# Output part of test-time training: VectorE's three chains of a step woven into each other, and the turn of the block's norm moved behind the output projection

## The reference, cut to what matters

```
Z1_bar = xq @ W1_s - eta_mb * Attn1 @ grad + b1_bar     # Attn1 = tril(xq @ xk.T)
out = xq + _ln(Z1_bar, ln_w, ln_b)                      # norm over the 8 features of a head
...
out = _ln(out, post_norm_weight, post_norm_bias)        # "post norm", over 256 features
return out @ o_w.T                                      # output projection
...
x = _layernorm(x + _L0_attn_ref(x, ...), axis=-1)       # the block's norm, over 256 features
```

## Time and profile before

| what | value |
|---|---|
| median of 3 runs | 1165.35 us |
| the three runs | 1157.6, 1166.76, 1165.35 us |
| span of the profiled execution (first to last instruction) | 1158.9 us |
| share of the span busy: TensorE, weight load, VectorE, ScalarE, GpSimd | 91%, 57%, 73%, 50%, 23% |
| first score matmul of step 0 | 169.31 us |
| first matmul of the next stage | 306.36 us |
| mean granted TensorE clock over the span | 0.975 |

### The profile page before, as it was taken

The page is one execution under the profiler, slowest core; times in us unless marked ns, Lnnn a source line. Parts: engine busy times, 40 slices in busy tenths (PEclk is TensorE's granted clock), DMA queues, the critical chain, the costliest instruction groups (busy, mean ns, idle before and its releaser), DMA issues. The chain is left out here.

```text
span 1158.9 us, 24222 instructions
## 1 busy us (share of the span) xinstructions
PE 1055.9 (91%) x8933; PEld 656.8 (57%) x8947; DVE 840.8 (73%) x1995; ACT 579.6 (50%) x1574; POOL 268.3 (23%) x331
## 2 busy tenths in 40 slices
PE   9799989999899999898999978899999998899965
PEld 5467757777433333354555457677777776444432
DVE  3699978999868778589984997854487878833326
ACT  2446444544267667654442336477777775322212
POOL 5201001111201112224422110410000001167742
PEclk9999999999899999999999989999999999999977
DMA  6833332000222221710000002940000000869567
GB/s 194 138 92 103 107 108 77 2 2 2 74 64 88 83 82 56 124 36 1 1 1 1 2 1 99 304 135 20 19 20 20 24 20 23 255 174 229 86 132 276
DMA packets 79200, 94.82 MB, mean 82 GB/s; under 512 B 17504, under 2 KB 61478, under 8 KB 78822
## 3 DMA queue, kind: packets, MB, share of 16 engines
q1 hardware_dynamic: 69356, 78.67, 23.8%
q0 software_dynamic: 6496, 9.57, 4.4%
q10 hardware_dynamic: 3232, 5.03, 1.2%
HBM read 68.65 MB, written 21.97 MB: 78 GB/s over the span
## 5 line engine op out<-in xcount | busy, mean ns | idle before, releaser
L533 DVE TENSOR_REDUCE gqa_x_slots<-banks 128x8 f32<-128x1024 f32 x64 | 78.4, 1226 | 28.9 <-PE banks L424 19.7
L490 ACT ACTIVATE gqa_expT<-banks 128x1024 f32<-128x1024 f32 x64 | 65.6, 1025 | 50.6 <-PE banks L445 50.6
L1752 ACT ACTIVATE mla_probs<-mla_scores,mla_neg_max 128x128 f32<-128x128 f32 x256 | 90.5, 386 | 0.1
L786 PE MATMUL banks<-ff_x_parts,ff_w_gate_up 128*128 128x512 bf16 x370 | 87.6, 384 | 1.9 <-PEq L348 1.2
L1825 DVE TENSOR_REDUCE mla_neg_max<-mla_scores 128x8 f32<-128x1024 f32 x32 | 39.2, 1225 | 64.9 <-PE mla_scores L1650 38.5
L445 PE MATMUL banks<-gqa_x_slotsT,gqa_keys 32*128 32x512 f32 x256 | 73.7, 646 | 13.2 <-issue 4.0
L424 PE MATMUL banks<-gqa_keys_bd,xT 32*128 32x512 f32 x256 | 72.6, 653 | 0.6 <-DVE gqa_x_slots L533 0.3
L1640 PE MATMUL mla_q_ps<-xT,mla_merged_home 128*128 128x128 f32 x512 | 62.4, 275 | 0.0
L786 PEld LDWEIGHTS banks<-ff_x_parts,ff_w_gate_up 128*128 128x128 bf16 x384 | 37.8, 99 | 42.5 <-issue 3.4
L1677 PE MATMUL mla_out_ps<-mla_merged_home,mla_attT 128*128 128x256 f32 x256 | 60.7, 380 | 0.7 <-ACT mla_attT L1766 0.7
L1640 PEld LDWEIGHTS mla_q_ps<-xT,mla_merged_home 128*128 128x128 f32 x512 | 59.7, 192 | 0.0
(11 more groups left out here) (448 smaller groups left out, 2580.4 us busy)
## 6 DMA issues: line engine op xcount, KB each, us to landing
gqa_keys_bd<-in_gqa_keys_bd SPq DMA_DIRECT2D x16, 512.0 KB, 3.4
moe_w_gu<-in_moe_w_gu SPq DMA_DIRECT2D x14, 384.0 KB, 5.7
moe_w_dn<-in_moe_w_down SPq DMA_DIRECT2D x24, 192.0 KB, 5.8
moe_sums<-moe_zeros SPq DMA_DIRECT2D x2, 2176.0 KB, 10.4
ba_attended<-in_moe_w_gu SPq DMA_DIRECT2D x10, 384.0 KB, 4.6
x_tok<-in_mla_kv_wo SPq DMA_DIRECT2D x8, 320.0 KB, 3.8
ttt_by_token<-ttt_g_pairs SPq DMA_DIRECT2D x4, 576.0 KB, 4.7
ttt_lanes<-ttt_by_token SPq DMA_DIRECT2D x16, 144.0 KB, 6.1
```

The lines of the kernel that those rows point to most:

```text
L490: nc.scalar.activation(expT[:, k % 2, 2 * u:2 * u + 2, :], scoresT, ACT.Exp, scale=HD ** -0.5).then_inc(exp_ready, 1)
L533: nc.vector.tensor_reduce(x_slots[:, b % 2, :, c * NJ + 2 * half:c * NJ + 2 * half + 2, HD].rearrange("p g j -> p j g"), scores[:, of].rea ...
L786: ins = nc.tensor.matmul(tile[:, n % 2], w_up[:, c, k, f * P:(f + 1) * P], x_parts[:, g % 2, part, c, :], start=(c == 0 and part == 0), st ...
L1752: ins = nc.scalar.activation(probs[:, k % NB, e, i, :], scores[:, k % 2, e, i, :], ACT.Exp, bias=neg_max[:, k % 2, e, i:i + 1], accum_out= ...
```

## The change

VectorE's step is written out by hand. Two methods are added to `Order`: `mark` raises the semaphore and returns the count to wait for, `after` waits for such a count. So the instruction that makes a result and the one that needs it can stand apart, and instructions of the other two chains stand between them. The head norm's chain moves ahead of masks 3 but for its last three instructions; the variance's reduction moves ahead of masks 2; the post norm is written ahead of the block norm's variance, and the block norm is written behind masks 2. The product with gamma is taken before the product with the reciprocal root. `added` and step 16's `block_norm` get a wait for `norm.turn_copied`, and `residual`'s wait becomes `resT_copied` in place of `resT_ready`.

TensorE issues `norm.tensor(b-3)` in unit 3, behind `last.out(b-2)`, and no longer in unit 2 ahead of `last.turn_res(b-2)` (but for b = 16, where it stays in unit 2, behind `turn_res`). ScalarE's order becomes `deviation`, `copy_res`, `norm.scalar`. No instruction that computes is added or dropped.

```
+    def mark(self, ins):
+        ins.then_inc(self.sem, 1)
+        self.k += 1
+        return self.base + self.k
+    def after(self, count):
+        self.eng.wait_ge(self.sem, count)
...
-                    if b == B + 1:
+                    if live(b - 2):
                         deviation(b - 2)
+                    if live(b - 3):
+                        last.copy_res(act, b - 3)
                     if live(b - 4):
                         norm.scalar(act, b - 4)
-                    if live(b - 3):
-                        last.copy_res(act, b - 3)
-                    if live(b - 2) and b != B + 1:
-                        deviation(b - 2)
...
                         if u == 2 and b == B:
                             last.turn_res(pe, b - 2)
-                        if u == 2 and live(b - 3):
+                        if u == 2 and live(b - 3) and b == B:
                             norm.tensor(pe, b - 3)
...
                         if u == 3 and live(b - 2) and b < B:
                             last.out(pe, b - 2)
+                        if u == 3 and live(b - 3) and b < B:
+                            norm.tensor(pe, b - 3)
...
                         post_stats(b - 2)
+                        need(dve, norm.turn_copied, b - 3)
                         block_norm(b - 3)
...
+                    masks(b, 0)
+                    if live(b - 2):
+                        need(dve, q_read, b - 1)
+                        post_summed = order.mark(nc.vector.bn_stats(last.stats[:], res))
+                    if live(b - 3):
+                        if b == 3:
+                            dve.wait_ge(x_loaded, 16)
+                        need(dve, last.out_ready, b - 2)
+                        need(dve, norm.turn_copied, b - 3)
+                        added = order.mark(norm.added(b - 3, last.out_of(b - 3)))
+                    if live(b - 2):
+                        order.after(post_summed)
+                        nc.vector.memset(last.spare[:], 0.0)
+                        post_spread = order.mark(nc.vector.bn_aggr(last.mean_var[:], last.stats[:]))
+                    if live(b - 3):
+                        order.after(added)
+                        summed = order.mark(nc.vector.bn_stats(norm.stats[:], norm.total))
+                    if live(b - 2):
+                        order.after(post_spread)
+                        ts(last.var_eps[:], last.mean_var[:, 1:2], last.EPS, None, ALU.add).then_inc(last.post_var_ready, 1)
+                    masks(b, 1)
+                    if live(b - 3):
+                        order.after(summed)
+                        nc.vector.memset(norm.spare[:], 0.0)
+                        spread = order.mark(nc.vector.bn_aggr(norm.mean_var[:], norm.stats[:]))
+                    if live(b - 2):
+                        post_norm(b - 2)
+                    if live(b - 3):
+                        order.after(spread)
+                        ts(norm.var_eps[:], norm.mean_var[:, 1:2], LN_EPS, None, ALU.add).then_inc(norm.var_ready, 1)
+                    if live(b - 1):
+                        need(dve, squared, b)
+                        tr(var[:], sq[:], AX_X, ALU.add).then_inc(var_ready, 1)
+                    masks(b, 2)
+                    if live(b - 1):
+                        need(dve, var_ready, b)
+                        order.mark(ts(head_var_eps[:], var[:], 1.0 / HD, EPS, ALU.mult, ALU.add))
+                        need(dve, std_ready, b)
+                        root = order.mark(nc.vector.reciprocal(rstd[:], std[:]))
+                        need(dve, z_kept, b)
+                        order.mark(tt(z[:].rearrange("p h d -> p (h d)"), z[:].rearrange("p h d -> p (h d)"), gamma_row[:], ALU.mult))
+                        order.after(root)
+                        half_square = order.mark(stt(spare_h[:], rstd[:], -0.5, rstd[:], ALU.mult, ALU.mult))
+                    if live(b - 3):
+                        need(dve, norm.rstd_ready, b - 2)
+                        need(dve, norm.kept, b - 3)
+                        need(dve, norm.turn_ready, b - 3)
+                        ts(norm.normed, norm.total, norm.mean_var[:, 0:1], norm.rstd[:], ALU.subtract, ALU.mult).then_inc(norm.norm_ready, 1)
+                    if live(b - 1):
+                        order.after(half_square)
+                        step_of = order.mark(tt(spare_h[:], spare_h[:], head_var_eps[:], ALU.mult))
+                    masks(b, 3)
+                    if live(b - 1):
+                        order.after(step_of)
+                        order(stt(rstd[:], spare_h[:], 1.5, rstd[:], ALU.add, ALU.mult))
+                        order(tt(z[:], z[:], wide(rstd), ALU.mult))
+                        need(dve, last.resT_copied, b - 1)
+                        need(dve, q_ready, b)
+                        tt(res, z[:].rearrange("p h d -> p (h d)"), q_tok_ps, ALU.add).then_inc(q_read, 1)
```

## The result

| | before | changed |
|---|---|---|
| median of 20 runs each, us | 1165.87 | 1158.75 |
| ratio to before (95% interval) | | 0.9942 (0.9924 to 0.9960) |
| span of the profiled execution, us | 1158.9 | 1160.2 (its own time 1162.08) |
| first score matmul of step 1 to the first matmul of the next stage, us | 173.50 to 306.36 = 132.86 | 175.83 to 303.50 = 127.67 |

The kernel became 0.6% faster, between 4.7 and 8.9 us. I had forecast 2.7 us. The time lies in the range, but the gain was about twice what I wrote (1.7 to 3.3 times), and most of what follows is about where that came from.

The account below looks back on a forecast made before the run. VectorE was taken to bound the step at 8.4 us, with TensorE needing 8.25. Gains of 1.0 (steps 3 to 15), 0.5 (step 2) and 1.2 (stage's end) made 2.7 us: 1165.35 to 1162.6, range 1154.5 to 1168.0 with run scatter.

Parts of the forecast that it names:

- The bound: Middle steps: VectorE sets 8.4 us, TensorE would need 8.25, so only about 0.15 us a step can be cashed.
- 11 x 0.12 = 1.3 us: VectorE's step: eleven of 14 waits for its own results go, each worth 0.12 us.
- 7.95 + 0.37 = 8.32: TensorE's new step: `norm.tensor` at 7.95 plus 0.37 to the next scores; range 8.25 to 8.48, against 8.40.
- 0.5 + 1.2: Stage's ends: 0.5 us gained in step 2 (0.3 to 0.6), 1.2 at step 16 and the end (0.9 to 1.6).
- the two cases that I had weighed: Stage's end, half-speed stretch behind step 16's stand: if it goes too, 1.6 us in all; if it stays, 0.9.
- The clock rival: Half-speed stretches here and in the next stage: 7 us less gives 3.5 us more than forecast, 1159.1; chance 0.1.
- The steps' own range: Whole kernel, without the scatter of runs: 1161.2 to 1165.2 us, a gain of 0.2 to 4.2.
- The slow rival: ScalarE's queue: a late reduction holds `copy_res` behind `deviation`, then `out` and TensorE wait; 5.2 us lost, 1167.9; chance 0.07.

Follow-up runs that it names:

- moves_only: Changed kernel with VectorE's old program (new waits kept) and `deviation` behind `copy_res`; TensorE's order as changed: 1164.97 us, ratio to before 1.0005.
- waits_at_once: Changed kernel with VectorE's new instruction order, but each own result waited for at once: 1160.99 us, ratio to before 0.9959.
- weave_only: Changed kernel with `norm.tensor` back ahead of `turn_res` and `norm.scalar` back ahead of `copy_res`: 1210.63 us, ratio to before 1.0329.
- after_again: Changed kernel once more with no edit, for a second profile and a comparison on one chip: 1159.35 us, ratio to before 0.9949.
- deviation_late: Changed kernel with ScalarE's `deviation` (square root) back behind `copy_res`: 1167.33 us, ratio to before 1.0000.

## Why the prediction was right in direction and too small in size

**The bound: right.** VectorE's own instructions set 8.4 us, TensorE would need less. Shown from both sides: the move alone leaves 8.42 (`moves_only`), and with the weave VectorE waits 1.02 us a step for TensorE.

**VectorE, "11 x 0.12 = 1.3 us": right.** `waits_at_once` puts these waits back, but for one (the block norm row's own wait stays away, the one behind `added` comes back), and VectorE needs 1.3 us a step more. What it had to spare in the changed kernel is nearly used up. The rows' reading (0.33 against 0.45) held, and the rule of the Trainium skill (VectorE: DVE Perf Modes, "The DRAIN you can't avoid"), that chains take as long with semaphores as without, did not hold for the instructions of 0.42 us here: 0.12 us each. That the time is nevertheless nearly the same with and without these waits is not that rule; it is TensorE's bound.

**TensorE's step, "7.95 + 0.37 = 8.32": this is the term that was mis-sized.** It measured 8.16, outside the 8.25 to 8.48 that I had given it. Up to `out` every offset was right to 0.01; the two spacings behind it were 0.96 and 0.31 in place of 1.06 and 0.37. I took `out` to scores for `out` to transposes, and gave as its other end a duration (1.13) on the longer side only. The lower side was left open, and it was there: the spacing between two groups belongs to the pair of neighbours, not to the first of them. Steps 3 to 15 gained 2.85 + 0.23 = 3.1 us, not 1.0.

**The ends of the stage, "0.5 + 1.2": 0.6 and 1.5.** Step 2 went from 8.54 to 7.95. In step 16 the stand went, and the clock stayed at 2.4 GHz, the better of the two cases that I had weighed: from the start of `apply(15,2)` to the hand-over it is 9.09 us before (297.27 to 306.36) and 7.58 after (295.92 to 303.50). In two profiles this stand is long (0.88 us before, 0.66 in `moves_only`), and the clock fell to half about 2 us behind it; in none of the eight in which it was gone or at most 0.6 us did it fall between the stand and the hand-over. `weave_only`, with its stands in every step, is left out of this count. That the stand is the cause is the likely reading of these rows, but it was not tested by itself. A window of `moves_only`, at 0.52:

```profile
302.10:305.50 3.40, 3.40 (x9) 1.75 (x8) 3.12 (x11) 0.73 (x3) 0.94 (x2) 0.52 0.00 0
```

**The sum.** 3.1 + 0.6 + 1.5 = 5.2 us in the stage, which lies in the interval of 4.7 to 8.9. The middle of that interval is 1.6 us more. Nothing outside the stage has changed, and single profiles differ by 4 us behind it. The clock rival had 1159.1, next to the measured 1158.75, but the clocks on record do not bear it out: among the runs that the ratio of `after_again` uses, the mean granted clock was 0.9743 changed and 0.9736 before, some 2 us less at half speed out of 60. That is worth 1 us and lies within the scatter. (The one stretch of 3.4 us that went with the stand of step 16 is already in the 1.5.) The mean times of these runs differ by 5.5 us, close to the stage's 5.2. So most of the 1.6 us is likely scatter, though this is not shown for the batch of the main result.

That the time lies between 1154.5 and 1168.0 was no proof of the sum: this range was the scatter of the runs, and no gain at all would have been inside it too. The steps' own range, a gain of 0.2 to 4.2 us, did not hold the 5.2 us of the stage, because the lower end of TensorE's step was left out of it.

**The slow rival: right as a mechanism, wrong in its side.** I feared that `deviation` ahead of `copy_res` could hold up `out`. In the step whose first scores start at 230.64 the square root (line 2842) ends at 235.88, and ScalarE then stands 0.77 us until `copy_res` (line 271) can start:

```profile
235.56 0.32 ACT L2842 ACTIVATE ttt_std<-ttt_var,ttt_eps 128x32 f32<-128x32 f32 x1
236.66 0.81 ACT L271 ACTIVATE rows<-banks,ttt_post_b,ttt_post_w 128x128 f32<-128x128 f32 x2 [0.77 <-PE banks L264]
```

And it is needed there: behind `copy_res` it makes the step 8.54. What I did not see at all is how close the weave is to a real loss: with `norm.tensor` left in place the kernel is 3.3% slower.

**What I missed in the trace of before.** Two groups of 16 matmuls stand next to each other at its first step, timeline of TensorE:

```profile
172.16 1.42 PE L2899 MATMUL banks<-ttt_g_pairs,ttt_masked 128*64 128x16 f32 x32
173.50 1.09 PE L2864 MATMUL banks<-ttt_q_bd,ttt_k_feat 32*64 32x256 f32 x16
```

1.34 us for 32, and 0.83 for 16 a few steps on the earlier trace rows. Read, it would have shown both why my spacings were unsafe and that TensorE had 0.3 us a step left in its order.

## What to carry to other kernels

Where two engines are both nearly full, find the one that only waits for itself, and then work out what the other needs: that is all that can be cashed. When a chain is woven later into a step, every consumer of its results on the other engines has to move as well; here one pair of transposes left in place (with its copy on ScalarE) turned a gain of 0.6% into a loss of 3.3%. Price a reordering on TensorE by pairs of neighbours, from start to start, each pair from a row that has exactly this pair.

## What the runs showed of the hardware that I had not expected

- The same 32 fp32 matmuls of `apply` take 1.34 to 1.35 us up to the next instruction in one group, and 1.61 us (0.78 + 0.83) in two groups with two transposes between, without any wait.
- With a stand of 1.0 us in each step (9.30 us at full clock) TensorE was granted 1.2 GHz for 82 of the stage's 174.5 us in `weave_only` (0.50 from 221 to 231), and the stage lost some 34 us on top of the stands' own 13. With 0.16 to 0.33 us lost to a wait in each step (0.16 before, 0.27 in `moves_only`, 0.33 in `deviation_late`) it stayed at 2.4 GHz through the middle of the stage.
- A wait of VectorE for its own last result costs 0.12 us behind an instruction of 0.42 us. With eleven of them in a step and TensorE as the bound, they cost nothing in the middle of the stage, and 0.7 us at its two ends.
